# DLRM tower with a compressed interaction network: splits moved from VectorE to GpSimd and to transfers, part of the first layer in three fp32r passes

## The chip, the cores and the metric

One core of a Trainium2 chip runs the whole kernel. The metric is the device time of one execution in microseconds (us), the median of several runs.

## The reference, cut to what matters

For 1024 batch rows, 39 table lookups of 16 floats each give `e` (batch 1024, 39 fields, depth 16). Two layers follow, each an outer product with the fields and a weighted sum, with bias and relu:

```python
x1 = relu(einsum('bhd,bmd,shm->bsd', e, e, W1) + b1)    # W1 (128, 39, 39)
x2 = relu(einsum('bhd,bmd,shm->bsd', x1, e, W2) + b2)   # W2 (128, 128, 39)
z = concat([x1.sum(-1), x2.sum(-1)])                    # (1024, 256)
y = relu(relu([z, dense_ctx] @ W_top1 + b) @ W_top2 + b) @ W_top3   # 272 -> 512 -> 256 -> 1
```

## The kernel before, in words

The batch is cut into 32 **tiles** of 32 rows. With the depth of 16 a tile is 512 columns, 4 blocks of 128 positions. A tile is worked off in two **pairs** (64 in all), and a pair has two blocks (`sub` 0 and 1).

**Lookups (GpSimd, L334 to L341).** Ten indirect DMAs per tile (one of them brings a row for each of 128 partitions) fill `looked`, a ring of 8 tiles. 30 are issued ahead of everything, then 6 in each pair, in three steps between GpSimd's sums.

**Placement and splits.** The looked-up rows have to move from one partition quarter to another into `e`: 16 copies per tile (`put_in_place`), on VectorE and ScalarE for the first two tiles, after that on ScalarE (`put`, L455), for one, two or four tiles at a time (`FILLS`, L35). Then ScalarE writes the high part of `e` in fp32r (L472), VectorE multiplies 15 rows out (`products`, L570), ScalarE writes their high part (L481), VectorE subtracts for the low parts (`low_part`, L580 and L583). TensorE turns the tile around (`turn`, L678) and ScalarE evacuates it into `x0t` (L432).

**First layer (TensorE, steps v = 0 to 6 of a tile).** The squares trick: `expand` (L690) selects sums of two fields into the staging bank BK_T, ScalarE squares them into `z1` (L444), and `layer1` (L702) multiplies by `w1_sb` in plain fp32, which the trace records as two instructions, into the bank BK_ACC1. There are six such chunks per tile and one fp32r product `wz` (L697). ScalarE and VectorE then make `x1h`, `x1` and `x1l` (L450, L453, L595). `expand`, the turns, the sums and the top MLP all share BK_T, one after another.

**Second layer.** For each pair 39 fields in 10 banks of up to 4 fields. A bank is 2 blocks by 3 fp32r matmuls of 512 columns (L724, L725, L726). 7 banks ("D", 27 fields) are drained by VectorE, which multiplies each field by the embedding and adds it into `acc` (L634, 54 instructions of 128x128 per pair). 3 banks ("A", 12 fields) are drained by ScalarE into `fy` (L425), and GpSimd adds these up with the bias (L348) into `fsum(p)`, which is the addend of VectorE's first instruction in pair p. The order of the banks is written out by hand in `ORDER` (L57): slots 0 to 9 of a pair are D D A D D A D D A D. The A banks belong to the pair ahead. Three double banks form a ring: bank n waits until bank n-3 is drained (L718). Two instructions of VectorE (L651, L655) close a pair, and GpSimd sums `x1` over positions (L380) once per tile.

**Steps in slots.** `layer1_steps` (L113) puts the steps of tile t into every second slot, from the second slot of an odd pair; `turn_step` (L140) puts the turn of tile t into slot 0 of pair 2t-3. Each engine's program runs in order, so a wait holds up everything behind it on that engine.

**Top MLP.** In three groups of batch rows (`GROUPS`, L73), the first two inserted into the slots at tiles 17 and 29, and the third, of 128 rows, after the last pair. **SP** issues the loads and the final store; after the loads of the MLP's weights it waits for the end.

Of the kernel before, what the change touches and what calls it, by code (L numbers as in the profile page):

```python
# [14 lines left out]
P = 128  # L15
# [19 lines left out]
FILLS = [(t, 1) for t in range(8)] + [(t, 2) for t in range(8, 20, 2)] + [(t, 4) for t in range(20, TILES, 4)]  # L35
FILL_OF = {t: f for f, (first, n) in enumerate(FILLS) for t in range(first, first + n)}
FILL_AT = {first: f for f, (first, n) in enumerate(FILLS)}

# [5 lines left out]
C1 = -(-(SHIFTS * M - ZP) // K1)  # L44

# [12 lines left out]
EARLY = 1  # L58
SLOTS = len(ORDER)
# [10 lines left out]
LOOKUPS_PER_PAIR = 6  # L70
FIRST_TILES = 2

GROUPS = ((0, 512), (512, 896), (896, 1024))  # L73
# [9 lines left out]
def bank_order():  # L83

    slots = [[("A", 0, a) for a in range(A_BANKS)] + [("A", 1, a) for a in range(EARLY)]]
    for p in range(PAIRS):
# [26 lines left out]
def layer1_steps(p, s):  # L113

    slot = SLOTS * p + s
    if 2 * slot <= C1:
        return [(1, v) for v in (2 * slot, 2 * slot + 1) if v <= C1]
    t, k = divmod(slot - 11, TILE_SLOTS)
    t += 2
    return [(t, k // 2)] if t < TILES and k % 2 == 0 and k // 2 <= C1 and slot >= 11 else []  # L120


def put_by_dve(f):

    return (0, 1) if f < FIRST_TILES else ()


def put_by_act(f):
    return tuple(k for k in range(Q) if k not in put_by_dve(f))


def puts_dve(f):
    return Q * sum(len(put_by_dve(g)) for g in range(f + 1))


def puts_act(f):
    return Q * sum(len(put_by_act(g)) for g in range(f + 1))


def turn_step(p, s):  # L140

    t = p // 2 + 2
    return t if p % 2 == 1 and s == 0 and t < TILES else None


def sums_step(p, s):

    return p // 2 - 1 if p % 2 == 0 and p and s == 6 else None
# [3 lines left out]
for g, tile in ((0, 17), (1, 29)):  # L152
    for c, s in enumerate((0, 4, 14, 16)):
        MLP_AT[TILE_SLOTS * tile + s] = (g, 1, c)
    for c, s in enumerate((0, 4)):
        MLP_AT[TILE_SLOTS * (tile + 1) + s] = (g, 2, c)
    MLP_AT[TILE_SLOTS * (tile + 1) + 14] = (g, 3, 0)
# [27 lines left out]
def cin_tower(nc, table, ids_first, ids, first_row, w1a, w1b, fold, w2, b2, sel, ident, rows_sum, wt1, wt1c, bt1, wt2, bt2, wt3, ctx_t, out):  # L185
    with ExitStack() as stack:
# [22 lines left out]
        wz = sb("wz", [P, S], F32R)  # L209
        fold_sb = sb("fold_sb", [K1, C1, M])  # L210
# [4 lines left out]
        z1 = sb("z1", [P, 2, N])  # L215
        x1 = sb("x1", [S, 2, N])
# [18 lines left out]
        hid1 = sb("hid1", [P, F1 // P, N])  # L235
        hid2 = sb("hid2", [P, F2 // P, N])
        y_sb = sb("y_sb", [1, B])
# [10 lines left out]
        s_look = [sem(f"s_look{t}") for t in range(TILES)]  # L248
        s_put_act = sem("s_put_act")
        s_put_dve = sem("s_put_dve")  # L250
        s_eh = sem("s_eh")
        s_el = sem("s_el")
        s_selr = sem("s_selr")
# [9 lines left out]
        s_prod = sem("s_prod")  # L263
        s_wzh = sem("s_wzh")
        s_wz = sem("s_wz")
        s_z1 = sem("s_z1")
        s_mm1 = sem("s_mm1")
# [22 lines left out]
        def put_in_place(f, k, q):  # L290

            t, n = FILLS[f]
            at = t % LOOKED
            return (e[q * BT:(q + 1) * BT, t:t + n, k:M:Q, :],
                    looked[k * BT:(k + 1) * BT, at:at + n, 0:len(range(k, M, Q)), q * DT:(q + 1) * DT])

        def filled(f):

            t, n = FILLS[f]
            return slice(t, t + n), slice(t % LOOKED, t % LOOKED + n)  # L300
# [11 lines left out]
        with nc.Block() as block:  # L312
            @block.sync
            def _(sp):
# [14 lines left out]
                sp.dma_start(out, y_sb[:]).then_inc(s_out, 16)  # L329
# [3 lines left out]
            def _(pool):  # L333
                def look_up(n):  # L334
                    t, j = divmod(n, LOOKUPS)
                    if j == 0 and t >= LOOKED:
                        pool.wait_ge(s_put_act, puts_act(FILL_OF[t - LOOKED]))
                        pool.wait_ge(s_put_dve, puts_dve(FILL_OF[t - LOOKED]))
# [23 lines left out]
                def last_fields(p):  # L362
# [6 lines left out]
                    if p >= 2:  # L369
                        pool.wait_ge(s_stt, stt_count(p - 2, 0))  # L370
                    added(p, j + 3, j, fsum[:, h, :, :], fy[:, h, :, 0, :], fy[:, h, :, 1, :])
# [22 lines left out]
                position_sum(0)  # L394
                first_fields(1)
                n = LOOKUPS_FIRST
                for p in range(PAIRS):
                    share = LOOKUPS_PER_PAIR
                    for j in range(1, A_BANKS):
# [3 lines left out]
                        n += step  # L403
                        if p + 1 < PAIRS:
# [6 lines left out]
                    n += step  # L411
                    if p + 2 < PAIRS:
# [3 lines left out]
            def _(act):  # L416
# [17 lines left out]
                def square(t, v):  # L434
# [9 lines left out]
                    nc.scalar.activation(z1[:, k % 2, :], src, ACT.Square).then_inc(s_z1, 1)  # L444
# [10 lines left out]
                def put(f, part, parts):  # L455

                    t, n = FILLS[f]
                    if part == 0:
                        act.wait_ge(s_look[t + n - 1], 16 * LOOKUPS)
                        for before in range(t, t + n - 1):  # L460
                            act.wait_ge(s_look[before], 16 * LOOKUPS)
                    copies = [(k, q) for k in put_by_act(f) for q in range(Q)]
                    for k, q in copies[len(copies) * part // parts:len(copies) * (part + 1) // parts]:
                        nc.scalar.activation(*put_in_place(f, k, q), ACT.Copy).then_inc(s_put_act, 1)  # L464

                def high_part(f):
                    tiles, at = filled(f)
                    act.wait_ge(s_put_act, puts_act(f))
                    act.wait_ge(s_put_dve, puts_dve(f))
                    if tiles.start >= LOOKED:  # L470
                        act.wait_ge(s_full, STAGED["turn", tiles.stop - 1 - LOOKED] + 1)
                    nc.scalar.activation(e_hl[:, at, 0:M, :].bitcast(F32R), e[:, tiles, :, :], ACT.Copy).then_inc(s_eh, 1)  # L472

                def products_high(f):
                    tiles, at = filled(f)
                    if f == 0:
                        act.wait_ge(s_ones, 1)
                    act.wait_ge(s_prod, f + 1)
                    src = prod[:, at, :].rearrange("p t (m d) -> p t m d", d=DT)
                    for row in (ZH, ZW):  # L480
                        nc.scalar.activation(e_hl[:, at, row:row + ZP, :].bitcast(F32R), src, ACT.Copy).then_inc(s_eh, 1)  # L481
# [23 lines left out]
                put(0, 0, 1)  # L505
# [6 lines left out]
                put(1, 0, 1)  # L512
                high_part(1)
                products_high(1)
                for n, (_, p, j) in enumerate(BANK_SLOTS[0]):
                    scaled_fields(p, j)
                    if n == 2:
                        turned(1)
                for p in range(PAIRS):
                    fill = FILL_AT.get(p // 2 + 2) if p % 2 == 0 else None  # L520
                    for s in range(SLOTS):
# [11 lines left out]
                        if fill is not None and s in (1, 3, 4):  # L533
# [351 lines left out]
```

## Time and profile before

| | before |
|---|---|
| median of 3 runs | 1227.49 us (1227.45 to 1227.75) |
| the profiled execution, its own time | 1228.31 us |
| its span, first to last instruction | 1226.4 us |
| TensorE busy | 1172.4 us (96%) |
| VectorE busy | 1005.4 us (82%) |
| GpSimd busy | 864.8 us (71%) |
| ScalarE busy | 672.1 us (55%) |
| granted TensorE clock, mean | 0.992 of full |

Busy time of an engine is the union of its instructions. Consecutive matmuls overlap in the records (one lasts 0.39 us while the next starts 0.23 us after it), so what one costs is read from start to start. The same holds for VectorE: 343 ns recorded, about 0.26 us from one to the next.

### The profile page before, as it was taken

The page shows a single profiled execution, that of the slowest core. Times are in us where ns is not written, and L with a number is a line of the kernel's source. Part 1 is how long each engine was busy: PE and PEld are TensorE (multiplying, and loading weights), DVE is VectorE, ACT ScalarE, POOL GpSimd, SP SyncE. Part 2 cuts the span into 40 slices and gives each one's busy share as a digit, 9 for nine tenths or more (in the row PEclk, how much of TensorE's full clock was granted, in tenths as well). Part 3 has the DMA queues.
Part 4 walks back from the last instruction along what each step waited for, and adds up shares of the span by engine and source line. Part 5 has one row for each costly group of instructions (what it writes and reads, how often), then busy time and mean ns, then how long its engine had stood idle before and what let it go on. Part 6 is the DMA issues. An engine that isn't in the chain of part 4 may idle for free.

```text
span 1226.4 us, 17749 instructions
## 1 busy us (share of the span) xinstructions
PE 1172.4 (96%) x4784; PEld 879.4 (72%) x4784; DVE 1005.4 (82%) x3692; ACT 672.1 (55%) x2188; POOL 864.8 (71%) x836
## 2 busy tenths in 40 slices
PE   3899999999999999999999999999999999999996
PEld 2577777777777777777776667777777777777775
DVE  4298898888899888888896678888888888887695
ACT  2656666665565656556564465555655565545430
POOL 7888878888888788788776757888886454444350
PEclk9899999999999999999999999999999999999997
DMA  5000000000000000000000000000000000000000
GB/s 177 5 4 4 4 4 3 4 4 5 3 4 3 4 3 3 4 4 3 4 4 3 3 3 3 4 3 4 3 4 2 1 1 1 1 1 1 1 1 1
DMA packets 12801, 9.08 MB, mean 7 GB/s; under 512 B 6190, under 2 KB 11822, under 8 KB 12573
## 3 DMA queue, kind: packets, MB, share of 16 engines
q0 software_dynamic: 10240, 2.64, 2.6%
q1 hardware_dynamic: 2461, 5.31, 1.3%
q8 instruction: 38, 0.62, 0.2%
q14 instruction: 62, 0.51, 0.1%
HBM read 7.92 MB, written 0.00 MB: 6 GB/s over the span
## 4 chain that ended last, share of the span: by engine, by line
PE 72%; DVE 18%; ACT 5%; issue 2%; POOL 2%; DMA 0%; SPq 0%; ACTq 0%
PE ps L724 17%; PE ps L726 17%; PE ps L725 17%; DVE acc L634 15%; PE ps L702 13%; PE ps L690 3%; PE ps L755 3%; ACT e L464 2%; ACT fy L425 2%; POOL looked L339 2%; DVE x1l L595 1%; PE ps L678 1%; DVE e_hl L580 1%; PE ps L697 0%; DVE e_hl L583 0%
## 5 line engine op out<-in xcount | busy, mean ns | idle before, releaser
L634 DVE SCALAR_TENSOR_TENSOR acc<-ps,e,acc 128x128 f32<-128x128 f32 x3200 | 854.4, 343 | 155.7 <-PE ps L726 152.4
L724 PE MATMUL ps<-w2h,x1h 128*128 128x512 f32 (+1 forms) x1280 | 582.4, 455 | 24.9 <-ACT fy L425 13.8
L348 POOL TENSOR_TENSOR fy<-fy 128x512 f32<-128x512 f32 (+1 forms) x256 | 403.0, 1574 | 214.3 <-ACT fy L425 193.5
L425 ACT ACTIVATE fy<-ps,e 128x128 f32<-128x128 f32 x1536 | 418.1, 387 | 198.8 <-PE ps L726 198.3
L726 PE MATMUL ps<-w2h,x1l 128*128 128x512 f32 (+1 forms) x1280 | 495.4, 387 | 0.0
L725 PE MATMUL ps<-w2l,x1h 128*128 128x512 f32 (+1 forms) x1280 | 494.3, 386 | 0.0
L339 POOL DMA_INDIRECT looked<-in_table,rows x320 | 310.9, 972 | 79.1 <-issue 55.0
L724 PEld LDWEIGHTS ps<-w2h,x1h 128*128 128x128 f32 x1280 | 241.5, 189 | 134.1 <-DVE acc L634 50.9
L725 PEld LDWEIGHTS ps<-w2l,x1h 128*128 128x128 f32 x1280 | 241.6, 189 | 82.6 <-issue 44.7
L726 PEld LDWEIGHTS ps<-w2h,x1l 128*128 128x128 f32 x1280 | 240.7, 188 | 48.4
L444 ACT ACTIVATE z<-ps 128x512 f32<-128x512 f32 x192 | 117.9, 614 | 224.8 <-PE ps L690 219.5
L702 PE MATMUL ps<-z,w_sb 128*128 128x512 f32 x384 | 198.8, 599 | 0.0
L702 PEld LDWEIGHTS ps<-z,w_sb 128*128 128x128 f32 x384 | 73.4, 192 | 16.6 <-ACT z L444 1.7
L690 PE MATMUL ps<-x0t,sel_r 78*128 78x512 f32 x186 | 74.0, 398 | 2.7 <-ACT z L444 1.8
L464 ACT ACTIVATE e<-looked 32x40 f32<-32x40 f32 (+5 forms) x256 | 67.3, 263 | 13.7 <-DMA looked<-in_table,rows 7.8
L348 POOL TENSOR_TENSOR fy<-fy,b_sb 128x256 f32<-128x256 f32 x64 | 47.7, 746 | 18.8 <-ACT fy L425 17.8
L634 DVE SCALAR_TENSOR_TENSOR acc<-ps,e,fsum 128x128 f32<-128x128 f32 x128 | 38.8, 344 | 26.0 <-POOL fsum L348 16.8
L348 POOL TENSOR_TENSOR fsum<-fy 128x256 f32<-128x256 f32 x64 | 47.5, 743 | 10.8 <-POOL fy L348 4.4
L690 PEld LDWEIGHTS ps<-x0t,sel_r 78*128 78x128 f32 x186 | 34.9, 188 | 10.9 <-ACT z L444 3.5
L634 DVE SCALAR_TENSOR_TENSOR ps<-ps,e,acc 128x128 f32<-128x128 f32 x128 | 38.9, 350 | 0.0
L432 ACT ACTIVATE x0t<-ps 128x512 fp32r<-128x512 f32 x32 | 19.4, 605 | 30.5 <-PE ps L678 30.5
L678 PE MATMUL ps<-ident_sb,e_hl 128*128 128x128 f32 x128 | 20.9, 287 | 9.1 <-DVE e_hl L583 8.8
(64 smaller groups left out, 385.5 us busy)
## 6 DMA issues: line engine op xcount, KB each, us to landing
looked<-in_table,rows POOLq DMA_INDIRECT x320, 2.3
w_st<-in_w SPq DMA_DIRECT2D x1, 1728.0 KB, 10.2
wt_sb<-in_wt SPq DMA_DIRECT2D x2, 512.0 KB
w_st<-in_w SPq DMA_DIRECT2D x1, 768.0 KB, 6.3
w_sb<-in_w1a SPq DMA_DIRECT2D x1, 448.0 KB, 3.2
w1b_sb<-in_w1b SPq DMA_DIRECT2D x1, 448.0 KB, 3.8
sel_st<-in_sel SPq DMA_DIRECT2D x1, 234.0 KB
ids_sb<-in_ids SPq DMA_DIRECT2D x1, 150.0 KB, 4.9
```

The source lines that it names most:

```text
L339: nc.gpsimd.indirect_dma_start(looked[:, t % LOOKED, j, :], None, table, bass.IndirectOffsetOnAxis(rows[:, t, j:j + 1], 0)).then_inc(s_loo ...
L348: nc.gpsimd.tensor_tensor(out, a, b, ALU.add).then_inc(s_fsum, 1)
L425: nc.scalar.activation(fy[:, p % 2, sub, m - MD, :], ps[:, 2 * (nth % RING) + sub, k * S:(k + 1) * S], ACT.Copy, scale=emb(p, sub, m)).the ...
L444: nc.scalar.activation(z1[:, k % 2, :], src, ACT.Square).then_inc(s_z1, 1)
L464: nc.scalar.activation(*put_in_place(f, k, q), ACT.Copy).then_inc(s_put_act, 1)
L634: nc.vector.scalar_tensor_tensor(acc[:, sub, :] if m < MD - 1 else y, y, emb(p, sub, m), acc[:, sub, :] if m else fsum[:, p % 2, sub, :], ...
L690: nc.tensor.matmul(ps[:, BK_T, :], sel_r[:, v, :], x0t[0:2 * M, t % 2, :], start=True, stop=True).then_inc(s_full, 1)
L702: nc.tensor.matmul(ps[:, BK_ACC1, :], w1_sb[:, v, :], z1[:, k % 2, :], start=False, stop=(v == C1 - 1)).then_inc(s_mm1, 1)
L724: nc.tensor.matmul(y, x1h[:, t % 2, at], w2h[:, cols], start=True, stop=False)
L725: nc.tensor.matmul(y, x1h[:, t % 2, at], w2l[:, cols], start=False, stop=False)
L726: mm = nc.tensor.matmul(y, x1l[:, t % 2, at], w2h[:, cols], start=False, stop=True)
L755: mm = nc.tensor.matmul(y, w, x, start=(k == 0), stop=(k == len(terms) - 1))
```

## The change

- In 4 of the 6 chunks of the first layer (v = 0, 1, 2, 4) of the tiles 5 to 31, ScalarE squares twice: into `zh` (fp32r) and in place in the PSUM bank. VectorE subtracts the one from the other into `zl`, and TensorE makes three fp32r passes (`w1h zh`, `w1l zh`, `w1h zl`) in place of the fp32 one. The steps of these tiles are three slots apart, not two.
- From tile 2 on the 16 placements of a tile are SBUF to SBUF DMAs issued by SP (rows of 16 bytes, 36 to 40 floats for each of 32 partitions). ScalarE's copies go.
- From tile 2 on GpSimd multiplies out and subtracts (`multiplied_out`, `low_parts`), one tile at a time: three instructions of 128x60, 128x156 and 128x60.
- GpSimd issues 8 lookups in each of the pairs 0 to 3, 6 afterwards. The splits of tile t are in pair 2t-4 for t under 5, else 2t-5; its turn is in the pair after (slot 3 for tile 2, slot 0 for tiles 3 and 4, slot 4 from tile 5).
- In pairs 0 to 3 VectorE starts without `fsum` and adds it at the end of the pair, with one more instruction per block (`LATE`).
- At the start D banks and A banks alternate. ScalarE makes the high part of the A part of W2 and of W1. The first bank waits for `x1h` alone.
- The groups of the MLP are 512, 448 and 64 rows (before 512, 384 and 128), and lie in other slots. `hid1`, `hid2` and `y_sb` lie over `w2_st`.

```diff
+SOON = 5
+SPLIT = (0, 1, 2, 4)
+LATE = 4
-GROUPS = ((0, 512), (512, 896), (896, 1024))
+GROUPS = ((0, 512), (512, 960), (960, 1024))
...
+    for t in range(2, TILES):
+        at = TILE_SLOTS * (t - 2)
+        first, apart = (15, 1) if t == 2 else (at + 11, 2) if t < SOON else (at + 6, 3)
+        v, rest = divmod(slot - first, apart)
...
+def split_pair(t):
+    return 2 * t - 4 if t < SOON else 2 * t - 5
...
+    t = SPLIT_IN.get(p - 1)
+    return t if t is not None and s == (3 if t == 2 else 0 if t < SOON else 4) else None
...
+def lookups(p):
+    return 8 if p < 4 else 6
...
             @block.sync
...
+                for t in range(FIRST_TILES, TILES):
+                    sp.wait_ge(s_look[t], 16 * LOOKUPS)
+                    for k in range(Q):
+                        for q in range(Q):
+                            sp.dma_start(*put_in_place(t, k, q)).then_inc(s_put[t - FIRST_TILES], 16)
...
             @block.gpsimd
...
                 for p in range(PAIRS):
                     for j in range(1, A_BANKS):
...
+                        if j == 1 and p and mine is not None:
+                            multiplied_out(nc.gpsimd, mine)
                         if p + 1 < PAIRS:
                             more_fields(p + 1, j) if j < A_BANKS - 1 else last_fields(p + 1)
                     if p % 2 == 0 and p // 2 + 1 < TILES:
                         position_sum(p // 2 + 1)
...
+                    if mine is not None:
+                        low_parts(nc.gpsimd, mine)
                     if p + 2 < PAIRS:
                         first_fields(p + 2)
...
                 def square(t, v):
...
+                    if is_split(t, v):
+                        nc.scalar.activation(zh[:, k % 2, :], src, ACT.Square).then_inc(s_z1, 1)
+                        nc.scalar.activation(src, src, ACT.Square).then_inc(s_sq, 1)
...
+                def square_low(t, v):
+                    k = C1 * t + v
+                    dve.wait_ge(s_sq, splits(t, v))
+                    if k >= 2:
+                        dve.wait_ge(s_mm1, k - 1)
+                    nc.vector.tensor_tensor(zl[:, k % 2, :], ps[:, BK_T, :], zh[:, k % 2, :], ALU.subtract).then_inc(s_zl, 1)
...
                 def turn(t):
-                    pe.wait_ge(s_eh, 3 * FILL_OF[t] + 3)
-                    pe.wait_ge(s_el, 2 * FILL_OF[t] + 2)
+                    pe.wait_ge(s_eh, 3 * t + 3)
+                    if t < FIRST_TILES:
+                        pe.wait_ge(s_el_first, 2 * t + 2)
+                    else:
+                        pe.wait_ge(s_el, 2 * (t - FIRST_TILES) + 2)
...
                 def layer1(t, v):
...
+                    if is_split(t, v):
+                        nc.tensor.matmul(ps[:, BK_ACC1, :], w1h[:, v, :], zh[:, k % 2, :], start=False, stop=False)
+                        nc.tensor.matmul(ps[:, BK_ACC1, :], w1l[:, v, :], zh[:, k % 2, :], start=False, stop=False)
+                        pe.wait_ge(s_zl, splits(t, v))
+                        mm = nc.tensor.matmul(ps[:, BK_ACC1, :], w1h[:, v, :], zl[:, k % 2, :], start=False, stop=(v == C1 - 1))
```

## Rows read from the trace of the kernel before

**Rows 1.** The page: busy time, share of the span and instructions of each engine.

```profile
PE 1172.4 (96%) x4784; PEld 879.4 (72%) x4784; DVE 1005.4 (82%) x3692; ACT 672.1 (55%) x2188; POOL 864.8 (71%) x836
```

**Rows 2.** Timeline of TensorE (start, duration, engine, line) around one fp32 chunk.

```profile
606.57 1.02 PE L702 MATMUL ps<-z,w_sb 128*128 128x512 f32 x2
607.03 0.79 PE L724 MATMUL ps<-w2h,x1h 128*128 128x512 f32 x1
607.66 0.40 PE L725 MATMUL ps<-w2l,x1h 128*128 128x512 f32 x1
```

**Rows 3.** Timelines of ScalarE and TensorE, one stall of a second-layer bank.

```profile
627.36 3.16 ACT L464 ACTIVATE e<-looked 32x80 f32<-32x80 f32 x11
...
632.87 0.47 PE L724 MATMUL ps<-w2h,x1h 128*128 128x512 f32 x1 [0.93 <-ACT fy L425]
```

**Rows 4.** Timeline of VectorE, its first instructions of pairs 6, 32, 40, 58.

```profile
160.53 0.61 DVE L634 SCALAR_TENSOR_TENSOR acc<-ps,e,fsum 128x128 f32<-128x128 f32 x2 [0.31 <-PE ps L726]
...
620.19 0.61 DVE L634 SCALAR_TENSOR_TENSOR acc<-ps,e,fsum 128x128 f32<-128x128 f32 x2 [0.31 <-PE ps L726]
...
783.27 0.61 DVE L634 SCALAR_TENSOR_TENSOR acc<-ps,e,fsum 128x128 f32<-128x128 f32 x2 [0.31 <-PE ps L726]
...
1099.85 0.61 DVE L634 SCALAR_TENSOR_TENSOR acc<-ps,e,fsum 128x128 f32<-128x128 f32 x2 [0.31 <-PE ps L726]
```

**Rows 5.** Timeline of GpSimd over one tile (two pairs).

```profile
600.51 0.73 POOL L348 TENSOR_TENSOR fsum<-fy 128x256 f32<-128x256 f32 x1 [0.17 <-DVE acc L634]
...
602.01 0.46 POOL L380 TENSOR_TENSOR xt<-xs 128x128 f32<-128x128 f32 x1
...
604.61 0.95 POOL L339 DMA_INDIRECT looked<-in_table,rows  x1 [0.30 <-issue]
...
617.82 0.73 POOL L348 TENSOR_TENSOR fsum<-fy 128x256 f32<-128x256 f32 x1 [0.17 <-POOL fy L348]
...
626.28 3.84 POOL L348 TENSOR_TENSOR fy<-fy 128x1024 f32<-128x1024 f32 x2 [2.25 <-ACT fy L425]
...
632.80 2.72 POOL L348 TENSOR_TENSOR fy<-fy 128x512 f32<-128x512 f32 x2 [0.33 <-ACT fy L425]
635.69 0.77 POOL L348 TENSOR_TENSOR fsum<-fy 128x256 f32<-128x256 f32 x1 [0.17 <-POOL fy L348]
```

**Rows 6.** Timeline of GpSimd early on: the 30th lookup, fsum(1).

```profile
46.54 0.94 POOL L339 DMA_INDIRECT looked<-in_table,rows  x1 [0.30 <-issue]
...
70.50 0.77 POOL L348 TENSOR_TENSOR fsum<-fy 128x256 f32<-128x256 f32 x1
```

**Rows 7.** Timeline of TensorE: the turns of tiles 3 and 4.

```profile
106.46 0.63 PE L678 MATMUL ps<-ident_sb,e_hl 128*128 128x128 f32 x4
...
141.61 0.63 PE L678 MATMUL ps<-ident_sb,e_hl 128*128 128x128 f32 x4
```

**Rows 8.** VectorE: 46 instructions of the last pair (timeline); `x1l` (lines by form).

```profile
1198.76 11.97 DVE L634 SCALAR_TENSOR_TENSOR acc<-ps,e,acc 128x128 f32<-128x128 f32 x46
...
L595 DVE SCALAR_TENSOR_TENSOR x1l<-ps,x1h 128x512 fp32r<-128x512 f32 x32 | 21.8, 682 | 4.7 <-ACT x L453 4.7
```

**Rows 9.** Timelines of VectorE and GpSimd: a split of W2 and a lookup beside it.

```profile
25.44 3.76 DVE L590 SCALAR_TENSOR_TENSOR w2l<-w_st,w2h 128x3456 fp32r<-128x3456 f32 x1
...
25.83 4.18 POOL L339 DMA_INDIRECT looked<-in_table,rows  x1 [0.30 <-issue]
```

**Rows 10.** SP's timeline, one issue; the page: the lookups' queue and their landing.

```profile
20.70 0.43 SPq L327 DMA_DIRECT2D ctx_sb<-in_ctx_t  x1
...
q0 software_dynamic: 10240, 2.64, 2.6%
...
looked<-in_table,rows POOLq DMA_INDIRECT x320, 2.3
```

**Rows 11.** Lines by form: matmuls of the MLP, 512 and 384 columns.

```profile
L755 PE MATMUL ps<-hid,wt_sb 128*128 128x512 f32 x16 | 7.2, 592 | 0.0
...
L755 PE MATMUL ps<-hid,wt_sb 128*128 128x384 f32 x16 | 5.5, 486 | 0.0
```

More of the change, by code:

```diff
@@ L83, in bank_order @@
 def bank_order():
-    slots = [[("A", 0, a) for a in range(A_BANKS)] + [("A", 1, a) for a in range(EARLY)]]
-    for p in range(PAIRS):
+    slots = [[("A", 0, 0), ("D", 0, 0), ("A", 0, 1), ("D", 0, 1), ("A", 0, 2)]]
+    first = (("D", 0, 2), ("D", 0, 3), ("A", 1, 0), ("D", 0, 4), ("D", 0, 5), ("A", 1, 1), ("D", 0, 6), ("A", 1, 2), ("A", 2, 0))
+    slots += [[bank] for bank in first] + [[]]
+    for p in range(1, PAIRS):
         d = a = 0
@@ L117, in layer1_steps, with is_split, splits, split_after @@
         return [(1, v) for v in (2 * slot, 2 * slot + 1) if v <= C1]
[L118 to L137, printed above, removed]
+    for t in range(2, TILES):
+        at = TILE_SLOTS * (t - 2)
+        first, apart = (15, 1) if t == 2 else (at + 11, 2) if t < SOON else (at + 6, 3)
+        v, rest = divmod(slot - first, apart)
+        if rest == 0 and 0 <= v <= C1:
+            return [(t, v)]
+    return []
+def is_split(t, v):
+    return t >= SOON and v in SPLIT
+def splits(t, v):
+    return sum(is_split(u, w) for u in range(t + 1) for w in range(C1) if (u, w) <= (t, v))
+def split_after(p, j):
+    slots = [s for s, kind in enumerate(ORDER) if kind == "D"] + [SLOTS]
+    return [at for s in range(slots[j], slots[j + 1]) for at in layer1_steps(p, s) if is_split(*at)]
+PUT_DVE, PUT_ACT = (0, 1), (2, 3)
+def split_pair(t):
+    return 2 * t - 4 if t < SOON else 2 * t - 5
+SPLIT_IN = {split_pair(t): t for t in range(2, TILES)}
 def turn_step(p, s):
-    t = p // 2 + 2
-    return t if p % 2 == 1 and s == 0 and t < TILES else None
+    t = SPLIT_IN.get(p - 1)
+    return t if t is not None and s == (3 if t == 2 else 0 if t < SOON else 4) else None
+def lookups(p):
+    return 8 if p < 4 else 6
 def sums_step(p, s):
-    return p // 2 - 1 if p % 2 == 0 and p and s == 6 else None
+    return p // 2 - 1 if p % 2 == 0 and p and s == 5 else None
 MLP_AT = {}
[L152 to L157, printed above, removed]
+for g, tile, at in ((0, 17, (0, 8, 11, 14, 20, 28, 34)), (1, 30, (8, 11, 14, 17, 20, 23, 27))):
+    for s, step in zip(at, [(1, c) for c in range(F1 // P)] + [(2, c) for c in range(F2 // P)] + [(3, 0)]):
+        MLP_AT[TILE_SLOTS * tile + s] = (g, *step)
 def mlp_step(p, s):
@@ L248, in cin_tower @@
         s_look = [sem(f"s_look{t}") for t in range(TILES)]
+        s_put = [sem(f"s_put{t}") for t in range(FIRST_TILES, TILES)]
         s_put_act = sem("s_put_act")
@@ L252, in cin_tower @@
         s_el = sem("s_el")
+        s_el_first = sem("s_el_first")
         s_selr = sem("s_selr")
@@ L394, in _ @@
                 position_sum(0)
+                multiplied_out(nc.gpsimd, 2)
                 first_fields(1)
@@ L397, in _ @@
                 for p in range(PAIRS):
-                    share = LOOKUPS_PER_PAIR
+                    share, mine = lookups(p), SPLIT_IN.get(p)
                     for j in range(1, A_BANKS):
@@ L453, in first_layer @@
                     nc.scalar.activation(x1[:, t % 2, :], ps[:, BK_ACC1, :], ACT.Relu, scale=0.5).then_inc(s_x1, 1)
[L455 to L476, printed above, removed]
-                        act.wait_ge(s_ones, 1)
-                    act.wait_ge(s_prod, f + 1)
-                    src = prod[:, at, :].rearrange("p t (m d) -> p t m d", d=DT)
+                def put(t):
+                    act.wait_ge(s_look[t], 16 * LOOKUPS)
+                    for k in PUT_ACT:
+                        for q in range(Q):
+                            nc.scalar.activation(*put_in_place(t, k, q), ACT.Copy).then_inc(s_put_act, 1)
```

205 lines of the change are left out of this document (121 added, 84 removed).

## The prediction

> **What bounds the kernel now.** I read the page's busy times first [rows 1]: TensorE 96%, VectorE 82%, GpSimd 71%. But 96% is a union of overlapping records, so I went to TensorE's timeline and read from start to start. A pass of 512 columns takes 0.23 us there, an fp32 chunk more: from the start of L702 to that of L725 are 607.66 - 606.57 = 1.09 us, and one pass of L724 lies in between, which leaves 0.86 us [rows 2]. With such prices a tile costs TensorE: 18 banks of 6 x 0.2285 = 24.7, two of 384 columns 2.1, six chunks 5.2, seven fp32r products 1.6, turn and sums 0.6, in all 34.2 us. What the tile really takes comes from VectorE's first instruction of each second pair: pairs 6 to 32 are 13 tiles in 620.19 - 160.53 = 459.7 us, 35.36 us each [rows 4]. So TensorE is the bound, and 1.1 us per tile are stalls. One of 0.93 us is a bank that ScalarE drains late, after 11 placement copies [rows 3].
>
> GpSimd is nearly as full. From fsum to fsum, with the waits for ScalarE taken out, it works 618.55 - 601.24 = 17.3 us in the pair with position sums and 636.46 - 618.55 - 2.25 - 0.33 = 15.3 us in the other [rows 5]. That is 32.6 us of 35.4, though the page's 71% suggests more air, since the 0.30 us between two lookups isn't counted as busy.
>
> **The change part by part.**
>
> *Three passes for one fp32 chunk.* 3 x 0.2285 = 0.69 us against 0.86 [rows 2]: 0.175 us saved, 0.70 us per tile of four. TensorE's own work becomes 33.5 us.
>
> *Placements leave ScalarE.* The stall of 0.93 us [rows 3] goes, and with it most of the excess over TensorE's work. ScalarE gets four more squares per tile, at slots three apart, where it has room.
>
> *VectorE.* Its loop instruction comes every (11.97 - 0.34)/45 = 0.258 us [rows 8]; 112 of them and `x1l` are 29.6 us per tile. Four subtractions of 512 columns, priced as `x1l` at 0.68 us [rows 8], give 32.3 us. They could be a little cheaper or dearer (two operands of another kind of instruction): 0.5 to 0.9 us, 31.6 to 33.2 in all. I laid the slots of a tile side by side with these prices: the ring holds TensorE up once, by some 0.3 us, after the banks of slots 10 and 11. So TensorE's pace is 33.9 to 34.1 us.
>
> *GpSimd's splits.* 128 columns take 0.46 us [rows 5] and 256 take 0.73 to 0.77, so 156 take some 0.52 and 60 some 0.31; with 0.1 us between instructions that is 0.4 us for `multiplied_out` and 1.1 for `low_parts`. 32.6 + 1.5 = 34.1 us, a little more with the new waits. So while lookups last (to pair 46) GpSimd and TensorE bind together: I take 34.2 us, and 34.0 afterwards. If they cost half of that, TensorE's 33.9 is left; if double, 35.6.
>
> *Placements by transfers.* 480 DMAs on SP's queue, which is otherwise idle there. An issue takes 0.43 us, about 0.46 from start to start [rows 10]: 7.4 us per tile of 34, hidden. Unshown is what rows of 16 bytes cost. The lookups' queue was busy 2.6% of 16 engines' 1226 us for 40960 rows of 64 bytes [rows 10], 0.012 us each, or 0.05 us for each of the 10240 packets. 4992 rows per tile on 16 engines are 3.9 us at the one price and 15.6 at the other; both fit into a tile's period. I take the lower, as it is a price per row too. The Trainium skill ("DMA: Bandwidth & Descriptors", Specifications) has transfers below 512 bytes go by read-modify-write; no row here shows it within SBUF.
>
> *VectorE no longer reads two SBUF tensors beside GpSimd.* At the start a lookup took 4.18 us, not 0.94, while VectorE wrote `w2l` from two SBUF operands [rows 9]. The Trainium skill ("GPSIMD Engine Reference", Specifications) says so: the two share SBUF interfaces when VectorE has two SBUF inputs. In the loop GpSimd's sums show no such stretching [rows 5], so I count no gain.
>
> *The first pairs: here the change loses.* GpSimd works through its queue in order. Before, it finished its 30 lookups at 47.5 us and fsum(1) at 71.3 [rows 6]. Now, before fsum(1), one more lookup (0.95 + 0.30 [rows 5] = 1.25) and the product of tile 2 (0.4) stand; that product waits for the transfers: lookups landed at 47.5 + 2.3, 16 issues 7.4, landing 2, so 59.2 against 57.9, when GpSimd is there; and pair 1's A banks now come behind more D banks (0 to 2.6, I take 1). fsum(1): 75. Then follow position sums 2.0, three lookups 3.8 and the low part 1.1: tile 2 can be turned at 82. fsum(2) is 17.3 + 2 x 1.25 + 1.1 later, at 96; fsum(3) 15.3 + 2.5 + 0.4 later, at 114; low part of tile 3 at 121. But its turn is in slot 0 of pair 3, which TensorE passed at 106.46 [rows 7]. TensorE stalls there, with all of the second layer behind it in its queue. The same again in pair 5: with fsum(4) at 137 and fsum(5) at 154, tile 4's low part is ready at 161, where its turn was at 141.61 [rows 7]. From then the distance to pair 6 is the old one (160.53 - 141.61 [rows 4, 7]): pair 6 starts near 180, **20 us late** (bounds 12 and 26: nothing but 7 extra lookups and two splits, or everything with the slower transfers). From tile 5 the turn is four slots later and meets no wait. `fsum` being added last in pairs 0 to 3 lets VectorE start 17 us earlier, but that time is not the bound: the chain on GpSimd is.
>
> *MLP.* 64 columns move from the last group to the second. Per matmul a column is (592 - 486)/128 = 0.8 ns [rows 11], 44 matmuls each: at most 2.3 us more in the second, which now lies where VectorE is the slower one and hides part, and at most 2.3 us less at the end, less if weight loads bind. I take -1 in all.
>
> **Sum**, against the span, 1226.4: pair 6 +20. Pairs 6 to 32: 13 x (34.2 - 35.36) = -15.1. Pairs 32 to 40, with the first MLP group: before 783.27 - 620.19 = 163.1 [rows 4]; now 4 x 34.0 + 20.5 = 156.5, -6.6. Pairs 40 to 58: before 316.6 [rows 4], now 3 x 34.2 + 6 x 34.0 = 306.6, -10.0. End -1. In all -12.7: 1213.7, as a run 1215.6 (1.9 lie around the span), and as a median 0.8 less: 1215.
>
> **The rivals.** (a) *The early stall is smaller*: if the low parts come out in time for turns 3 and 4 (fewer waits than I laid out), pair 6 is only 12 us late, and with 34.0 throughout the time is 1215 - 8 - 3 = 1204. For it: the new slots look laid out for the turns. Against: each term of the chain is a row. 25%. (b) *Slower: the subtraction on VectorE becomes the wait.* `square_low` stands in VectorE's queue behind one D bank and ahead of the next; at A slots it waits for TensorE's expand and two squares of ScalarE, and the bank behind it is drained late, which stops TensorE three banks on. VectorE has 34.0 - 32.3 = 1.7 us of air per tile for four such waits. At 0.6 us each it needs 34.7, where the late start is no longer won back (26 tiles, 1215 + 26 x 0.5 = 1228); at 0.8 us each it is 35.3 and the time 1242. For it: 82% busy before the added 2.7 us [rows 1]. 25%. (c) *16-byte rows are dear* (0.05 us): tile 2's placement lands 9 us later, GpSimd and all behind it too, some 1224. 8%. (d) *Three passes save nothing*, since the third waits for `zl`: +0.70 per tile to GpSimd-bound tiles is hidden up to 34.2, else 27 x 0.4 = 11, 1226. 2%. My forecast: 40%.
>
> **Numbers.** 1215 is the forecast's. It holds 1208 to 1222 alone (GpSimd's splits and the wait at pair 1). The range takes in (a) and half of (b): 1199 to 1236. 0.2%, 2.5 us, is what a measurement of this kernel can tell. Faster: (a), nearly all of my case, part of (c) = 0.70. Same 0.05. Slower: (b) 0.25.
>
> **What would show it.** In the changed profile: three passes 0.23 us apart in place of 0.86; TensorE idle before the turns of tiles 3 and 4, released by GpSimd's low part, some 10 and 6 us; VectorE's pair 6 near 180; then 34.2 us per tile, GpSimd without idle time before its sums, fsum shortly before VectorE's first instruction. Wrong if pair 6 comes before 172, if tiles take under 33.8 or over 34.7 us, or if TensorE's releaser in the loop is VectorE or `zl`.

## The result, and the profile after

The changed kernel takes 1231.22 us (1230.14 to 1233.35, 6 runs) against 1227.62 of the kernel before: a ratio of 1.0033, with a 95% interval from 1.0022 to 1.0043. It is 0.3% slower, where 1% faster was forecast. A second set of runs of it (a0 below) gave 1.0032 (1.0019 to 1.0044).

From the page of the kernel after, with the parts that answer to [rows 1]: busy times, the clock, VectorE's subtractions, and TensorE's first pass of each block of a bank, with the idle time before it.

```profile
span 1229.5 us, 18625 instructions
PE 1169.5 (95%) x4892; PEld 893.8 (73%) x4892; DVE 1043.3 (85%) x3763; ACT 658.8 (54%) x2103; POOL 892.5 (73%) x926
PEclk9989989999999999999999999999999999999997
L639 DVE TENSOR_TENSOR zl<-ps,zh 128x512 fp32r<-128x512 f32 x108 | 73.7, 682 | 4.9 <-ACT ps L509 3.5
L797 PE MATMUL ps<-w2h,x1h 128*128 128x512 f32 (+1 forms) x1280 | 534.3, 417 | 10.6 <-DVE acc L690 7.1
```

TensorE's busy time fell by 2.9 us and the span rose by 3.1. The granted clock dips in the third and the sixth slice; before it did so in the second alone. A subtraction takes 0.68 us, as priced. Of the 10.6 us that TensorE stands idle before first passes, 7.1 end with VectorE's draining; the prediction had named VectorE as releaser in the loop as a sign that it would be wrong.

VectorE's first instructions of pairs 6, 32, 40 and 58 (its timeline, as in [rows 4]) say where the time went.

```profile
184.96 0.61 DVE L690 SCALAR_TENSOR_TENSOR acc<-ps,e,fsum 128x128 f32<-128x128 f32 x2 [0.31 <-PE ps L801]
...
635.87 0.73 DVE L690 SCALAR_TENSOR_TENSOR acc<-ps,e,fsum 128x128 f32<-128x128 f32 x2
...
794.86 0.60 DVE L690 SCALAR_TENSOR_TENSOR acc<-ps,e,fsum 128x128 f32<-128x128 f32 x2
...
1106.50 0.60 DVE L690 SCALAR_TENSOR_TENSOR acc<-ps,e,fsum 128x128 f32<-128x128 f32 x2
```

Against [rows 4], stretch by stretch:

| stretch | before, us | after, us | difference | forecast |
|---|---|---|---|---|
| to pair 6 | 160.5 | 185.0 | +24.4 | +20 |
| pairs 6 to 32 (13 tiles) | 459.7 | 450.9 | -8.8 | -15.1 |
| pairs 32 to 40, first MLP group | 163.1 | 159.0 | -4.1 | -6.6 |
| pairs 40 to 58 (9 tiles) | 316.6 | 311.6 | -4.9 | -10.0 |
| the rest | 126.6 | 123.0 | -3.6 | -1 |
| span | 1226.4 | 1229.5 | +3.1 | -12.7 |

**The early loss** stands in TensorE's timeline, at the turns of tiles 2, 3 and 4. The column in brackets is idle time before the row. It says "issue", so the profile names no releaser; that it is GpSimd rests on the times below and on the experiment r1.

```profile
80.93 1.10 PE L741 MATMUL ps<-ident_sb,e_hl 128*128 128x128 f32 x4 [10.38 <-issue]
...
121.67 1.10 PE L741 MATMUL ps<-ident_sb,e_hl 128*128 128x128 f32 x4 [7.74 <-issue]
...
163.24 1.10 PE L741 MATMUL ps<-ident_sb,e_hl 128*128 128x128 f32 x4 [4.79 <-issue]
```

GpSimd's timeline has the second of its two low parts of the same three tiles.

```profile
80.51 0.32 POOL L351 TENSOR_TENSOR e_hl<-prod,e_hl 128x60 f32<-128x60 f32 x1
...
121.25 0.32 POOL L351 TENSOR_TENSOR e_hl<-prod,e_hl 128x60 f32<-128x60 f32 x1
...
162.82 0.32 POOL L351 TENSOR_TENSOR e_hl<-prod,e_hl 128x60 f32<-128x60 f32 x1
```

Each turn starts 0.1 us after the low part ends. The three waits are 22.9 us. There are three and not the two that the prediction laid out: the turn of tile 2 waits too. A turn then takes 1.10 us, not 0.63 as in [rows 7], and the first passes behind it go 0.43 us apart, not 0.23: TensorE has stood idle and runs at the lower of its two levels (1.2 GHz) at first. The windows view gives a granted clock of 0.92 for 97 to 142 us.

**The steady pace.** A tile takes 311.64/9 = 34.63 us where 34.0 to 34.2 was forecast. Here is VectorE's timeline over part of a tile.

```profile
1054.16 0.69 DVE L639 TENSOR_TENSOR zl<-ps,zh 128x512 fp32r<-128x512 f32 x1
1054.77 0.28 DVE L712 TENSOR_SCALAR p<-ps 128x128 f32<-128x128 f32 x1
1055.08 0.29 DVE L708 SCALAR_TENSOR_TENSOR p<-ps,p 128x128 f32<-128x128 f32 x1
1055.29 0.60 DVE L690 SCALAR_TENSOR_TENSOR acc<-ps,e,fsum 128x128 f32<-128x128 f32 x2
1055.81 3.70 DVE L690 SCALAR_TENSOR_TENSOR acc<-ps,e,acc 128x128 f32<-128x128 f32 x14
1059.42 0.68 DVE L639 TENSOR_TENSOR zl<-ps,zh 128x512 fp32r<-128x512 f32 x1
1060.02 4.21 DVE L690 SCALAR_TENSOR_TENSOR acc<-ps,e,acc 128x128 f32<-128x128 f32 x16
```

From 1054.2 to 1064.2 VectorE has no gap: two subtractions stand among its banks. In the middle of that stretch TensorE waits for it, as its timeline shows.

```profile
1059.56 0.50 PE L797 MATMUL ps<-w2h,x1h 128*128 128x512 f32 x1 [0.16 <-DVE acc L690]
```

This one gap is small (0.55 us from the pass before to this one, not 0.23). There is one of its kind per tile, 13 in the 13 tiles of pairs 6 to 32, and some three **hops**: passes that start 0.33 or 0.34 us after the one before. A hop leaves no idle time in the records, since a record lasts 0.39 us. Over these tiles an undisturbed pass of 512 columns takes 0.2265 us from start to start. All passes of the second layer that take over 0.245 us, the gap among them, put together 1.0 us per tile on top of that.

### The profile page after: what moved, and what is told of

It reads as the page before. It is cut to its first block, busy times and chain, and to the rows that moved or that the text cites. A ratio compares the mean times of both kernels' runs of the same rounds, so it can differ in the third digit from the quotient of the medians.

```text
span 1229.5 us, 18625 instructions
## 1 busy us (share of the span) xinstructions
PE 1169.5 (95%) x4892; PEld 893.8 (73%) x4892; DVE 1043.3 (85%) x3763; ACT 658.8 (54%) x2103; POOL 892.5 (73%) x926
## 3 DMA queue, kind: packets, MB, share of 16 engines
q1 hardware_dynamic: 159901, 7.73, 7.3%
## 4 chain that ended last, share of the span: by engine, by line
PE 73%; DVE 12%; ACT 7%; issue 5%; POOL 2%; DMA 0%; ACTq 0%; SPq 0%; DVEq 0%
PE ps L797 19%; PE ps L798 18%; PE ps L801 18%; DVE acc L690 11%; PE ps L771 5%; ACT fy L488 4%; PE ps L830 3%; PE ps L753 3%; POOL looked L395 2%; PE ps L741 1%; ACT zh L508 1%; PE ps L766 1%; PE ps L767 1%; PE ps L769 1%; ACT ps L509 1%
## 5 line engine op out<-in xcount | busy, mean ns | idle before, releaser
L797 PE MATMUL ps<-w2h,x1h 128*128 128x512 f32 (+1 forms) x1280 | 534.3, 417 | 10.6 <-DVE acc L690 7.1
L508 ACT ACTIVATE zh<-ps 128x512 fp32r<-128x512 f32 x108 | 67.6, 626 | 142.3 <-PE ps L753 142.3
L511 ACT ACTIVATE z<-ps 128x512 f32<-128x512 f32 x84 | 50.6, 603 | 141.7 <-PE ps L753 137.3
L771 PE MATMUL ps<-z,w_sb 128*128 128x512 f32 x168 | 86.9, 599 | 0.0
L639 DVE TENSOR_TENSOR zl<-ps,zh 128x512 fp32r<-128x512 f32 x108 | 73.7, 682 | 4.9 <-ACT ps L509 3.5
L509 ACT ACTIVATE ps<-ps 128x512 f32<-128x512 f32 x108 | 67.9, 629 | 0.0
L741 PEld LDWEIGHTS ps<-ident_sb,e_hl 128*128 128x128 f32 x128 | 21.0, 206 | 44.7 <-issue 44.5
L741 PE MATMUL ps<-ident_sb,e_hl 128*128 128x128 f32 x128 | 22.5, 304 | 30.5 <-issue 22.9
L766 PE MATMUL ps<-zh,w1h 128*128 128x512 f32 x108 | 42.9, 397 | 0.0
L767 PE MATMUL ps<-zh,w1l 128*128 128x512 f32 x108 | 42.7, 395 | 0.0
```

The source lines that it names most:

```text
L508: nc.scalar.activation(zh[:, k % 2, :], src, ACT.Square).then_inc(s_z1, 1)
L509: nc.scalar.activation(src, src, ACT.Square).then_inc(s_sq, 1)
L639: nc.vector.tensor_tensor(zl[:, k % 2, :], ps[:, BK_T, :], zh[:, k % 2, :], ALU.subtract).then_inc(s_zl, 1)
L771: mm = nc.tensor.matmul(ps[:, BK_ACC1, :], w1_sb[:, v, :], z1[:, k % 2, :], start=False, stop=(v == C1 - 1))
L797: nc.tensor.matmul(y, x1h[:, t % 2, at], w2h[:, cols], start=True, stop=False)
```

## The experiments

The runs were made in four sessions: r1 to r4, then a0 with r5 to r7, then r8 to r10, then r11. Ratios are against the kernel before, on the same chip in the same session. In the first and the third session pair 0 of every profile of the new kernels ends at 70 to 78 us, in the other two at 64 to 66. The kernel before was only 4 to 5 us longer there, so between sessions a ratio is off by some 0.2%, and what a change is worth is read from the length of stages. "Pairs 1 to 5" is the time from the end of VectorE's pair 0 to the end of its pair 5 (87.5 us in the kernel before), and "tile" the steady length of a tile, from the ends of VectorE's pairs 6 to 32.

| run | ratio (95% interval) | end of pair 0, us | pairs 1 to 5, us | tile, us |
|---|---|---|---|---|
| the changed kernel again, a0 | 1.0032 (1.0019 to 1.0044) | 64.7 | 119.0 | 34.65 |
| low parts sooner, r1 | 0.9938 (0.9922 to 0.9955) | 72.2 | 105.2 | 34.67 |
| early splits on VectorE, r2 | 0.9943 (0.9927 to 0.9960) | 77.5 | 100.4 | 34.67 |
| no passes, r3 | 1.0015 (1.0005 to 1.0024) | 72.0 | 119.6 | 34.50 |
| six lookups, r4 | 1.0055 (1.0038 to 1.0072) | 72.5 | 115.8 | 34.90 |
| no subtraction, r5 | 0.9933 (0.9916 to 0.9949) | 65.5 | 121.2 | 34.17 |
| r1 and r3 together, r6 | 0.9885 (0.9869 to 0.9902) | 64.3 | 105.3 | 34.51 |
| old slots, r7 | 0.9966 (0.9953 to 0.9978) | 64.7 | 98.2 | 35.12 |
| r8 | 0.9869 (0.9852 to 0.9885) | 70.7 | 100.4 | 34.50 |
| fsum last in pair 0 only, r9 | 1.0032 (1.0019 to 1.0044) | 73.4 | 119.7 | 34.64 |
| two chunks at D slots, r10 | 1.0066 (1.0050 to 1.0083) | 71.5 | 119.2 | 34.75 |
| r8 with two chunks at A slots, r11 | 0.9826 (0.9813 to 0.9840) | 65.0 | 101.1 | 34.39 |

### The baseline

> The changed kernel once more, on the same chip as the kernels it is compared with: 1.0033 of the kernel before, the end of pair 5 some 24 us after that of before, 34.65 us per tile from there. Each of the other runs is read against this one.

As expected, with waits of 10.1, 7.8 and 4.8 us before the three turns.

### Low parts sooner in GpSimd's queue

```diff
+                    if mine is not None and mine < SOON:
+                        low_parts(nc.gpsimd, mine)
                     if p % 2 == 0 and p // 2 + 1 < TILES:
                         position_sum(p // 2 + 1)
...
-                    if mine is not None:
+                    if mine is not None and mine >= SOON:
                         low_parts(nc.gpsimd, mine)
```

> For tiles 2, 3 and 4 GpSimd's low parts stand right behind the last sums of their pair, ahead of the position sums and of three or two lookups; nothing else is changed against the changed kernel. Theory G (the three turns wait for GpSimd's low part, which stands late in its queue): each low part comes 2.0 + 3.8 us earlier for tiles 2 and 3, 2.0 + 2.5 for tile 4, so TensorE's idle time before the three turns falls from 10.4, 7.7 and 4.8 us to about 4.6, 2 and 0.3, pair 6 starts 16 us sooner (near 168) and the time is 1231 - 16 = 1215. Rival R (the transfers of the rows, or the lookups, are what comes late): the idle times stay, 1231. Rival C (GpSimd's whole chain is the bound, the turn only shows it): the waits before the turns go, but VectorE waits for fsum at the start of pairs 4 to 6 instead, and the time stays above 1225.

The ratio fell by 0.0095, 11.6 us; pairs 1 to 5 fell from 119.0 to 105.2 us. Of the three waits two are left in TensorE's timeline of this run, the third is down to 0.5 us.

```profile
82.31 1.10 PE L743 MATMUL ps<-ident_sb,e_hl 128*128 128x128 f32 x4 [4.28 <-issue]
...
121.00 1.10 PE L743 MATMUL ps<-ident_sb,e_hl 128*128 128x128 f32 x4 [4.59 <-issue]
```

Same transfers, same lookups, two instructions of each of three tiles moved within one queue: the rivals R and C fall. The stage gives 14 us and not 16, because the second turn, reached sooner, still waits 4.6 us, not 2.

### Early splits back on VectorE

```diff
+                        soon = SPLIT_IN.get(p)
+                        if soon is not None and soon < SOON:
+                            if j == 4:
+                                multiplied_out(nc.vector, soon)
+                            if j == (6 if p == 0 else 5):
+                                low_parts(nc.vector, soon)
```

(These instructions are taken out of GpSimd's program, and their semaphores follow; that part of the diff is left out here.)

> The products and low parts of tiles 2, 3 and 4 alone go back to VectorE (after its banks 4 and 5 of their pairs, 6 for tile 2), the rest is the changed kernel. Theory G: no turn waits for GpSimd's queue, the three idle times of 10.4, 7.7 and 4.8 us go entirely; what is late next is fsum(4), which GpSimd has at about 134 because of its eight lookups a pair, so VectorE waits there some 8 to 12 us, and pair 6 starts near 168 in place of 184: 1231 - 15 = 1216. Rival R (transfers late): VectorE waits for the rows in its own queue, and the time is 1231 or more. If nothing on GpSimd is late next, the whole 23 us come back: 1208.

The turns no longer wait. What is late next is fsum(4), as VectorE's timeline of this run shows.

```profile
139.84 0.61 DVE L689 SCALAR_TENSOR_TENSOR acc<-ps,e,fsum 128x128 f32<-128x128 f32 x2 [3.98 <-POOL fsum L404]
```

It is a wait of 4.0 us, where 8 to 12 was expected. TensorE also waits 4.7 us for VectorE at 77 us, around the splits of tile 2, which are in pair 0 and make it longer here (77.5 us for 72 in the others of its session). By the ratio the gain is that of r1, 11 us.

### Six lookups, and fsum last only once

```diff
-    return 8 if p < 4 else 6
+    return 6
```

> Six lookups in each of the first four pairs too, in place of eight; the rest is the changed kernel. Theory G with the lookups as a part of the delay: GpSimd's low part of tile 2 comes 2.5 us sooner, of tile 3 some 6, of tile 4 up to 8, less what ScalarE then makes it wait; the idle times before the turns fall to about 8, 4 and 1, and the lookups of tile 5 are then issued only just before its product, which costs some 3 to 5 us in pair 5: 1231 - 10 + 3 = 1224. If the lookups were not part of the delay: 1231. If the later lookups cost more than they give (each tile's rows come late until they have caught up): 1235 or more.

The waits before the turns of tiles 2 and 3 fell to 7.4 and 5.2 us, that of tile 4 stayed at 4.8. But pair 6 then took 19.6 us and pair 8 19.4, where they took 18.9 and 18.0: the rows of tiles 5 and 6 came late. In GpSimd's timeline of this run the product of tile 5, at 180.5 us, has waited 10.5 us for them. Pairs 1 to 5 are 3.2 us shorter than in a0, pairs 6 to 32 4.1 us longer. So in sum it is a draw within 1 us, not the 7 us of gain that were expected; the higher ratio is mostly the session's. The eight lookups are a cost at one place and needed at the next.

```diff
-LATE = 4
+LATE = 1
```

> fsum is added last in pair 0 alone (LATE = 1 in place of 4), the rest is the changed kernel. Theory G (in the first pairs the turns that wait for GpSimd's low parts are the bound, fsum is there in time): eight instructions less per block on VectorE, fsum(1) is ready at 74.5 while TensorE stands before the turn until 80.9, fsum(3) at 115 before 121.7; fsum(2), ready at 95, is just in time: no change within 0.2%, at most 2 us worse. Rival (the late sums are what keeps the loss at 24 us): VectorE stands 7 us or more at the start of pair 1, and the time is 1238.

There was no change: pairs 1 to 5 take 119.7 us for 119.0, and the rest is the same. TensorE's timeline in this run:

```profile
84.99 0.80 PE L797 MATMUL ps<-w2h,x1h 128*128 128x512 f32 x1 [7.08 <-DVE acc L690]
89.14 1.10 PE L741 MATMUL ps<-ident_sb,e_hl 128*128 128x128 f32 x4 [1.22 <-issue]
```

VectorE does stand 9.4 us for fsum(1), as the rival had it, and TensorE 7.1 us for VectorE, but the turn behind it then waits 1.2 us and no longer 10. The same time is waited one step sooner. Adding fsum last in pairs 1 to 3 is worth nothing while the turns wait. (In pair 0 it can't be left out in this order of banks: with VectorE's bank second in the ring, the A banks that make up fsum(0) would never get one. That is read from the program and wasn't tried.)

### The passes

```diff
-SPLIT = (0, 1, 2, 4)
+SPLIT = ()
```

> No chunk is split: all six chunks of the first layer are plain fp32 as before, at the new spacing; no second square on ScalarE and no subtraction on VectorE; the rest is the changed kernel. Theory V (the subtractions on VectorE fill the time in which TensorE's ring would be drained, so three passes give back less than their 0.70 us per tile): a tile takes 34.4 to 34.8 us where the changed kernel takes 34.65, and the time is 1226 to 1235, no worse than 1231 by more than 4. Rival P (the passes give their full 0.70 us per tile, and the stalls have another cause): a tile takes 35.35 us, 27 tiles cost 19 us, and the time is 1250.

A tile takes 34.50 us without any three-pass chunk, less than the 34.65 with four. At these slots the passes with their subtractions give back nothing.

```diff
-                        for at in split_after(p, j):
-                            square_low(*at)
...
-                        mm = nc.tensor.matmul(ps[:, BK_ACC1, :], w1h[:, v, :], zl[:, k % 2, :], start=False, stop=(v == C1 - 1))
+                        mm = nc.tensor.matmul(ps[:, BK_ACC1, :], w1h[:, v, :], zh[:, k % 2, :], start=False, stop=(v == C1 - 1))
```

> Leaves out VectorE's subtraction for the four split chunks: the third pass multiplies zh once more in place of zl. TensorE's three passes and ScalarE's two squares stay; VectorE has 2.6 us less per tile. Theory V (with the subtractions VectorE drains the ring just too late, so the passes' gain is handed back): a tile takes 33.8 to 34.0 us in place of 34.65, the whole 27 x 0.7 = 19 us less, near 1212 or 0.988 of before. Rival S (the second square on ScalarE, or the passes' own pace, holds TensorE): a tile stays above 34.5, and the time within 3 us of the changed kernel's.

A tile takes 34.17 us. The first row below is the windows view (busy time and instructions of each engine, clock, DMA) of the changed kernel from 250 to 600 us, the second of this run.

```profile
250.00:600.00 350.00, 348.16 (x1506) 272.78 (x1505) 327.04 (x1183) 205.18 (x660) 300.67 (x314) 1.00 0.13 7
```

```profile
250.00:600.00 350.00, 350.00 (x1527) 278.02 (x1526) 309.01 (x1161) 206.08 (x661) 304.95 (x319) 1.00 0.13 7
```

VectorE goes from 93% busy (327.04 of 350) to 88%, and TensorE from 99.5% to 100%. (What this kernel computes is not the function any more; it serves for its time alone.) So of the 0.70 us that four trios should save, the passes save 0.33 (34.50 to 34.17), and the subtractions take 0.48 back (34.17 to 34.65). Theory V named the right engine, but both its sizes were off: 33.8 to 34.0 was not reached.

Where did the other 0.37 go? Start to start over pairs 6 to 32, an fp32 chunk costs 0.863 us, of which 0.405 stand in the pass behind it, and a trio of passes 0.699, where 3 x 0.2285 = 0.686 was priced; four of them save 0.655, so 0.05 is missing there. The other 0.32 is in the 108 passes of 512 columns of the second layer. Without those 0.405 they take 25.28 us per tile in r5 and 24.96 in r6, the kernel without three-pass chunks. It comes in two forms:

- *Hops*, 0.22 us. Passes over 0.245 us put 0.54 us per tile on top in r5 and 0.32 in r6. The new one is the start of a bank for which ScalarE's `fy` comes last: in each of the 13 tiles of r5 two passes in a row take 0.34 us there, in none of r6. So rival S is not empty: ScalarE, which squares twice, is late once per tile. That the second square is the reason is likely, but not shown.
- *Slower passes*, 0.10 us. In both kernels a pass takes 0.223 to 0.228 us or 0.229 to 0.240. Of the second passes of each block's three, which wait for nothing, 32% take over 0.2285 us in r6 and 54% in r5 (468 each, means 0.2284 and 0.2302). Behind an fp32 chunk the passes are back at 0.227 from the fourth on; behind a trio only from the ninth (51 places each, medians). The granted clock is 1.00 in both. Why they are slower there was not settled.

```diff
-SPLIT = (0, 1, 2, 4)
+SPLIT = (0, 1)
```

> Two chunks (v = 0 and 1) in three passes in place of four, the rest is the changed kernel. Known: 34.50 us per tile with none, 34.65 with four, 34.17 with four but without the subtractions. Theory V (each pass trio gives TensorE about 0.08 us and each subtraction costs 0.12): 34.55 to 34.6, the time within 0.15% of both neighbours. Rival T (only the chunks at A slots, v = 2 and 4, hold the ring up, those at D slots pay): 34.2 to 34.4 per tile, 1222, 0.4% under the kernel without passes.

34.75 to 34.78 us, slower than with none and than with all four: the two chunks at slots where VectorE has a bank of its own only cost, 0.25 us per tile for two subtractions of 0.68 us and after what their passes save. Rival T had the sign the wrong way round; theory V, by which all cost the same, falls too.

### What the transfers and the slots are worth

```diff
-SOON = 5
+SOON = TILES
-    return 8 if p < 4 else 6
+    return 6
+                        if j == A_BANKS - 1 and mine is not None:
+                            low_parts(nc.gpsimd, mine)
                         if p + 1 < PAIRS:
                             more_fields(p + 1, j) if j < A_BANKS - 1 else last_fields(p + 1)
...
-                    if mine is not None:
-                        low_parts(nc.gpsimd, mine)
```

> The placements by transfers and the splits on GpSimd stay, but all tiles from 3 on keep the steps and turns where the kernel before had them (two slots apart, turn in slot 0 of pair 2t-3), no chunk is split, every pair has six lookups, and GpSimd's low part stands ahead of its last sums, where ScalarE's high part has just been made. Theory G + V (the loss is the early schedule, the steady gain comes from the placements alone): no turn waits over 1 us, pair 6 starts within 3 us of before, a tile takes 34.3 to 34.7 us: 1227.5 + 2 - 28 x 0.85 = 1206, 0.982 of before. Rival: GpSimd's queue is now the bound in every tile (its 34.1 us plus waits for ScalarE's high part, which delay its sums): 35.0 us or more per tile while lookups last, 1220 or more.

Pair 6 starts at 163.2, 2.7 us after that of before, as expected: the early loss is gone. But a tile takes 35.12 us. GpSimd is not the cause, since in pairs 47 and later, when the lookups are over, it is the same 35.12. TensorE waits 0.5 us for VectorE once per tile (0.86 us from pass to pass, for 0.18), where one pair ends. So transfers and splits at the old slots give 35.36 - 35.12 = 0.24 us per tile in pairs 6 to 32, and only 35.18 - 35.12 = 0.06 in pairs 40 to 58. The kernel before shows why it is so little: from pair 12 on its tiles with placement copies in them take 36.0 us (later 36.2) and those without 34.9. The copies cost 1.1 us at a time, but r7 is 0.2 us longer than the tiles without copies; why is open.

The new **slots** give another 0.6 (35.12 to 34.51 in r6), since in r6 the wait at the pair's end is gone. Between r7 and r6 the steps go from two to three slots apart, but their first slot, the slot of the turn, the pair of the splits and the place of GpSimd's low parts change with it, so that the spacing alone does it isn't shown. I had put the gain down to ScalarE's copies and left the slots unpriced.

### Together

> Both at once: GpSimd's low parts of tiles 2 to 4 ahead of the position sums, and all chunks in plain fp32. If the early wait and the passes are separate terms, the gains add: 0.0095 from the one and 0.0018 from the other, so 1.0033 - 0.0113 = 0.992 of before, with 34.5 us per tile and turns that wait 4 to 5 us twice. If the passes' small loss was only noise of the run, it equals the low-first kernel, 0.994.

The ratio fell by 0.0147, not by 0.0113; the median is 1213.4 us. The two add up: against a0, in the same session, pairs 1 to 5 are 13.7 us shorter and all behind them 3.2. The 0.0113 was added up from ratios of the first session, which are off by the late start.

```diff
-SPLIT = (0, 1, 2, 4)
+SPLIT = ()
-    return 8 if p < 4 else 6
+    return 7 if p < 4 else 6
+                        if j == A_BANKS - 1 and mine is not None and mine < SOON:
+                            low_parts(nc.gpsimd, mine)
...
-                    if mine is not None:
+                    if mine is not None and mine >= SOON:
                         low_parts(nc.gpsimd, mine)
```

> Low parts of tiles 2 to 4 ahead of the last sums of their pair, seven lookups in the first four pairs in place of eight, all chunks in plain fp32, the rest as in the changed kernel. Theory G: the waits of 4.8 and 5.3 us that the low-first kernel still has before the turns of tiles 2 and 3 shrink to under 3, GpSimd is 5 us sooner by pair 4, and pair 5 ends at 164 to 166 in place of 169: 1209, 0.985 of before. Rival: GpSimd stands in its queue waiting for ScalarE's high part, its sums come later by as much, and the stall moves to fsum: pair 5 ends at 169 or later, 1213 or more.

0.9869, against 0.9885 for r6, with intervals that overlap. Pair 5 ended at 171.2 us, in a session where pair 0 ends some 6 us later, so near 165; pairs 1 to 5 take 100.4 us for 105.3. In place of the two turns one bank of ScalarE is late, by 6.0 us, and VectorE waits 1.6 and 2.2 us for fsum(4) and fsum(5).

```diff
-SPLIT = (0, 1, 2, 4)
+SPLIT = (2, 4)
```

> As the kernel r8 (low parts ahead of the last sums, seven lookups early), but the two chunks at slots of A banks (v = 2 and 4) go in three passes. Known per tile: 34.50 us without passes, 34.77 with v = 0 and 1, 34.65 with all four. If the two at A slots are the ones that pay (VectorE has no bank to drain in an A slot, so its subtraction finds free time), a tile takes 34.25 to 34.4 us, 3 to 7 us under r8: 0.981 to 0.985 of before. If every subtraction costs VectorE's ring the same wherever it stands, a tile takes 34.6 to 34.8 and the time is 0.989 to 0.992.

(The diff is against the changed kernel, on top of the edits of r8.) 0.9826, 1205.8 us: 2.1% below the changed kernel and 1.7% below the one before. A tile takes 34.39 us where r8 has 34.50. So the two chunks at A slots do pay, 0.11 us per tile. From the end of pair 0 on r11 is 2.8 us shorter than r8; that the ratios differ by 5 us fits the late start of r8's session. What is late now are the placed rows of tile 3: in ScalarE's timeline of this run the high part of that tile, at 101.7 us, has waited 8.6 us for them, and TensorE's next bank of ScalarE 6.1 us.

## Why the prediction was wrong

- **The first pairs** (right, undersized). The step "here the change loses" held: fsum(1) was ready at 74.5 us for 75, the low parts at 80.8, 121.6 and 163.1 for 82, 121 and 161. The loss is 24.4 us for 20. Two us of the rest are the last low part: fsum(4) and fsum(5) came at 140.4 and 158.0, for 137 and 154. The others are the distance from the turn to pair 6, which the sum took from the old trace. From the turn of tile 4 to the end of pair 5 it is 18.6 us before, 21.4 and 20.0 in two profiles of the changed kernel, and 18.7 in r1 and r6, where that turn hardly waits: a wait costs something behind it too, a part of it as passes at the lower clock.
- **The steady pace** (the step that failed). "TensorE's pace is 33.9 to 34.1": it was 34.65. Three terms of the sum were mis-sized. First, TensorE's own work without three-pass chunks was priced at 34.2 us; r6, in which it shows no idle time from 250 to 600 us, has 34.51, and 0.32 of that are hops that the records hide. Second, the passes save 0.33 us per tile in the loop, not 0.70, since the passes around them slow down and ScalarE comes late once; so "TensorE's own work becomes 33.5 us" is 34.17 in r5. Third, the four subtractions were said to hold the ring up once, by 0.3 us; without them the tile is 0.48 us shorter. Over the 26 tiles to pair 58, with the MLP, it is 14 us, nearly all of the 15.8 by which the sum is off. (The sum's own terms, 33.5 and 0.3, make 33.8; 33.9 to 34.1 was taken.)
- **GpSimd as a second bound** from pair 6 was wrong: the pace is the same with lookups (34.65) and without (34.63). Its splits cost what was estimated (0.53, 0.32 and 0.32 us each by lines), and its 34.1 us stay just below the 34.65.
- **Rival (b)** came true in kind: VectorE, with its subtractions, is what TensorE waits for in the loop. That its pace, 34.7, and its time, 1228, lie near the measured 34.65 and 1231 is in part luck. It reached them by four waits of 0.6 us, of which 1.7 us of air were taken off: 1.2 us above the 33.5 of TensorE's own work. Measured were 0.48 us, on top of 34.17; the rival did not have the two other terms, and they make up for what it had too large. It had 25%; the hand-made table of the slots, which left out how close VectorE and TensorE run, was trusted too far.
- **Rival (c)** fell: all of SP's queue took 7.3% of 16 engines' 1229.5 us, 0.009 us for each of 159901 packets, less than the lower price. The Trainium skill ("DMA: Bandwidth & Descriptors", Specifications) has transfers below 512 bytes go by read-modify-write; whether these runs of 16 bytes, SBUF to SBUF, do so, no run here shows, but all that they cost is within these 0.009 us.
- **The end** gave 3.6 us for 1. Of these 1.2 are behind the last pair, as forecast. The others are in the last six pairs, for which the sum had counted no steady gain at all; how much of them is the tiles' pace and how much the second MLP group was not separated.

## What to carry to other kernels

When work moves to an engine with a long program of its own, ask where in its queue the result will stand and which engine's program stops for it; a lower total on the engine relieved says nothing about that. Moving two instructions per tile, for three tiles, ahead of sums that nobody was waiting for was worth 14 us here. When a second engine is 93% busy, an instruction added to it is not hidden: the four subtractions of 0.68 us cost 0.12 us each, more than the 0.08 that each saved on the first engine. Try such an instruction only at slots where that engine has nothing of its own to drain: two at D slots cost 0.25 us per tile, two at A slots gained 0.11. And compare stages, not whole times, when runs come from different sessions.

## What was not expected of the hardware

fp32r passes of 512 columns that wait for nothing come in two groups, with means of 0.2265 and 0.233 us, at a granted clock of 1.00. The kernels differ in the share of the longer ones (26% to 33% in those without three-pass chunks, 38% to 56% in those with them), not in the two means.

And the start depends on the session, not on the kernel. In all seven profiles of the first and the third session (r1 to r4, r8 to r10) VectorE and ScalarE both stand still for 6 to 7 us, from about 42 us on, and what ends it is on no engine of the core's profile; in none of the other profiles do they. It isn't the chip alone: r11 ran on the same chip, by its number, as r1 to r4 and shows nothing of it. The kernel before took 1232.6 and 1231.4 us in these sessions instead of 1227 to 1228. The steady tile is unchanged. What it is stays open.
